# Unread full-height products on TensorE at the start of the two plain attentions of a two-layer kernel

## The chip, the cores and the metric

The kernel runs on one core of a Trainium2 chip. The metric is the device time of one execution, in microseconds (us). Five engines work side by side, each with an instruction list of its own: TensorE (PE: matrix products, with its weight loads shown as PEld), VectorE (DVE), ScalarE (ACT), GpSimd (POOL) and SyncE (SP, which here issues the DMAs). They wait for each other by semaphores. Products are written to PSUM, eight banks of 128 partitions x 512 fp32 values. TensorE's clock is granted at one of two levels, and the profile gives it as a share: 1.00 is 2.4 GHz, 0.50 is 1.2 GHz.

## The reference, cut to what matters

Two pre-norm layers follow each other over 2 x 1024 rows of 128 numbers. Each has an attention of 16 heads of 8 numbers and a mixture of experts. There are three attentions: the layer 0 attention (with rotary embedding), the layer 1 attention, and one with relative positions in the last block. The first two are the plain ones:

```python
scores = jnp.einsum('bqhd,bkhd->bhqk', q, k) * scale
attn = jax.nn.softmax(scores, axis=-1)
out = jnp.einsum('bhqk,bkhd->bqhd', attn, v)
```

With 2 sequences and 16 heads, a plain attention has 32 heads of 1024 x 1024 scores each, and the softmax subtracts each row's maximum.

## The kernel before

The program is one list of stages, the same on all engines: `front(0)` (norm and projections of layer 0), `attention(0)`, `front(1)`, the first experts, `front(2)`, `attention(1)`, `front(3)`, the relative attention, `front(4)`, the second experts. No scheduler moves anything: every engine runs its instructions in the order in which the code writes them, and a wait holds up all that stands behind it on its engine. Between `front(0)` and `attention(0)`, and between `front(2)` and `attention(1)`, there is no meeting of the engines, so each goes on as soon as its own list lets it.

Queries and keys are split into a high and a low part and stacked to 24 rows, stored to DRAM, and loaded head by head by SyncE (`load_qk`) into four slots, four times over in partition blocks of 32. A product of these stacks thus uses 24 or 25 of the 128 rows of the array (thin, below), and products in different blocks of 32 rows run side by side. A product that uses all 128 rows is called full-height.

On TensorE, `attention(a)` first waits for all projections to be read (`products_read`) and for the first head's stacks (`qk_in`). It then computes the scores of heads 0 and 1 ahead of everything else: `scores` (L671) is a pair of thin products of 512 columns each into two banks, for 128 queries against 1024 keys; eight such pairs make a head, 16 the two heads. VectorE takes the maximum of each row over the two banks (`row_max`, L1246) into `M`. The pairs alternate between banks 2, 3 and banks 4, 5, and each waits (`max_done`) until the maximum of the pair before the last is taken. Within head 1's pairs stands `max_row` (L678): a full-height product that turns head 0's maxima into a row. ScalarE copies the row (`MT`), SyncE sends it by DMA into row 24 of the queries' stack, and the head loop's first wait (`m_in`) is for this DMA.

The head loop then calls `position` (L700) for each head. It has eight tiles `kt`. In a tile TensorE computes a score pair of the head after the next (L671), the turned scores of this head with the maximum subtracted by row 24 (`turned`, L686, thin, two products into the ring of banks 0, 1 and 7), and, three tiles behind, the products with the values (`values`, L696: full-height, 256 columns of fp32, four groups of 32 output rows side by side, into columns 0 to 255 of bank 6). ScalarE takes the exponentials of the turned scores (L1529, two per tile). In tile 1 `max_row` turns the next head's maxima. In the first head (`first`) there are no values' products in tiles 0 to 2.

An fp32 product is run as two matmul instructions of two passes each, one of the stacks (whose type is fp32r) as one, so the views count two for a `max_row` and eight for a `values`.

Of the kernel before, what the change touches and what calls it, by code (L numbers as in the profile page):

```python
# [24 lines left out]
P = 128  # L25
# [62 lines left out]
def two_layers(nc, A, out):  # L88
    with ExitStack() as ctx:
        def sb(name, shape, dt=F32):  # L90
            return ctx.enter_context(nc.sbuf_tensor(name, shape, dt))
# [12 lines left out]
        PS = ctx.enter_context(nc.psum_tensor("PS", [P, 8, GW], F32))  # L104

        def bank(b, dt=F32):
            return PS[:, b, :] if dt == F32 else PS[:, b, :].bitcast(dt)
# [12 lines left out]
        ident = sb("ident", [P, P])  # L120
        w_qkv = sb("w_qkv", [P, 3, 5 * P])
# [435 lines left out]
        def _(e):  # L557
# [3 lines left out]
            def products_read(n):  # L561

                e.wait_ge(qin_ok, n)
                e.wait_ge(kin_ok, n)
                e.wait_ge(v_ok, n)
# [4 lines left out]
            def gates(g, bk):  # L570

                for t in range(GT):
                    m = transpose(PS[0:NE1, bk, t * P:(t + 1) * P], gate[:, GT * g + t, :])
                m.then_inc(gtp_ok, 1)

            def front(f):
# [79 lines left out]
                if f == 4:  # L656
                    e.wait_ge(gate_ok, 2)
                    for g in range(NG):
                        if g == NG - 1:
                            e.wait_ge(gate_ok, 3)  # L660
                        gates(g, GATE_BANK[g])

            def attention(a):
                HB = NH * a

                def scores(n, s, qt):

                    e.wait_ge(max_done, 8 * (HB + n) + qt + 1)
                    for kh in range(2):
                        rows_ = slice((2 + kh) * KR, (2 + kh) * KR + MROW)  # L670
                        m = e.matmul(bank(2 + 2 * (qt % 2) + kh), Qs_r[rows_, s, qt * P:(qt + 1) * P],  # L671
                                     Ks_r[rows_, s, kh * GW:(kh + 1) * GW], start=True, stop=True)
                    m.then_inc(s_done, 1)

                def max_row(n, s, alone=False):

                    e.wait_ge(max_done, 2 + 8 * (HB + n) + 8)
                    e.matmul(PS[0:QT, 6, 256:256 + P], M[:, s, :], ident[:], start=alone, stop=True,  # L678
                             skip_group_check=True).then_inc(mt_done, 1)

                def turned(n, s, x, turn):

                    e.wait_ge(exp_done, 16 * (HB + n) + x)
                    rows_ = slice(x % 2 * KR, x % 2 * KR + MROW + 1)
                    kt, qh = x // 2, x % 2
                    e.matmul(bank(RING[(x + turn) % 3]), Ks_r[rows_, s, kt * P:(kt + 1) * P],  # L686
                             Qs_r[rows_, s, qh * GW:(qh + 1) * GW], start=True, stop=True).then_inc(st_done, 1)

                def values(n, s, kt):
                    e.wait_ge(exp_done, 2 + 16 * (HB + n) + 2 * kt + 2)  # L690
                    if kt == 0:
                        e.wait_ge(v_ready, HB + n + 1)
                        if not (isinstance(n, int) and HB + n == 0):
                            e.wait_ge(o_copied, HB + n)
                    for g in range(4):
                        m = e.matmul(PS[32 * g:32 * g + VC, 6, 0:256], Va[:, s, kt, :],  # L696
                                     PR[:, kt % 4, g * 256:(g + 1) * 256], start=(kt == 0), stop=(kt == QT - 1))
                    m.then_inc(pv_done, 1)

                def position(n, block, s, turn, first=False, ahead=True, rows_next=True):  # L700

                    s2 = (s + 2) % SLOTS
                    e.wait_ge(m_in[s], 32 * (NH // SLOTS * a + block + 1))
                    for kt in range(QT):
                        if ahead:
                            if kt == 0:
                                e.wait_ge(qk_in[s2], 128 * (NH // SLOTS * a + block + (s >= 2) + 1))
                            scores(n + 2, s2, kt)
                        turned(n, s, 2 * kt, turn)
                        turned(n, s, 2 * kt + 1, turn)  # L710
                        if kt == 2 and rows_next:
                            e.wait_ge(mt_copied, HB + n + 2)
                        if kt >= 3:
                            values(n, s, kt - 3)
                        elif not first:
                            values(n - 1, (s - 1) % SLOTS, QT - 3 + kt)
                        if kt == 1 and rows_next:
                            max_row(n + 1, (s + 1) % SLOTS, alone=first)

                if a == 0:  # L720
                    e.sem_inc(exp_done, 2)
                    e.sem_inc(pv_done, 4)
                products_read(4 * (a + 1))
                for n in range(2):
                    e.wait_ge(qk_in[n], 128 * (NH // SLOTS * a + 1))
                    for qt in range(QT):
                        scores(n, n, qt)
                        if n == 1 and qt == 1:
                            max_row(0, 0, alone=True)
                e.wait_ge(mt_copied, HB + 1)  # L730
                position(0, 0, 0, 0, first=True)
                for n in range(1, NH):
                    position(n, n // SLOTS, n % SLOTS, n % 3, ahead=n < NH - 2, rows_next=n < NH - 1)
                for kt in range(QT - 3, QT):
                    values(NH - 1, SLOTS - 1, kt)
# [269 lines left out]
            def front2():  # L1005
                back(0)
                front(2)

            plan = [lambda: front(0), lambda: attention(0), lambda: front(1), experts0, front2,
                    lambda: attention(1), lambda: front(3), relative_attention, lambda: front(4), experts1]  # L1010
            for k, run in enumerate(plan):
                run()
# [943 lines left out]
```

## Time and profile before

| | |
|---|---|
| median of 3 runs | 2077.16 us (2076.91 to 2084.83) |
| the profiled execution | 2072.94 us |
| its span, first to last instruction | 2071.1 us |
| TensorE (PE) busy | 1926.4 us, 93% |
| VectorE (DVE) busy | 1376.6 us, 66% |
| ScalarE (ACT) busy | 1206.2 us, 58% |
| mean granted clock of TensorE | 0.952 |

How to read it: the shares of busy time are means over stages with different limits, and a matmul counts as busy while it waits inside the array, so they say little of one stage. What a change in one stage is worth is read from the stretch of the trace in which it lies: which engine is busy there without a break, and who waits for whom. A window of the trace gives for each engine its busy time and its number of instructions in that stretch, and then the mean granted clock. A line of the timeline gives the start, the time from the first start to the last end of a few like instructions in a row, the engine, the line of the code, and what is written from what; in brackets stands the idle time of the engine ahead of it and what ended that.

### The profile page before, as it was taken

Reading aid. Unit: us, or ns where it says so; the run is one execution under the profiler, and the core shown is the slowest. Engines: PE = TensorE matmul, PEld = TensorE weight load, DVE = VectorE, ACT = ScalarE, POOL = GpSimd, SP = SyncE. Lnnn points to the kernel's source line nnn. Section 1 sums busy time; section 2 is a strip of 40 time slices with the busy share of each in tenths; the row PEclk is TensorE's granted clock in tenths of the full one; section 3 lists DMA queues with packets and bytes.
Section 4 is the critical chain, followed back from the end, with each engine's and each line's share of the span. In section 5 each row is a group of like instructions: output and inputs, shape, how many; then the busy total and the mean of one; then the engine's idle time right before and its main releaser. Section 6 shows DMA issues by size and latency. Waiting matters only on the chain.

```text
span 2071.1 us, 40381 instructions
## 1 busy us (share of the span) xinstructions
PE 1926.4 (93%) x13792; PEld 1163.5 (56%) x13792; DVE 1376.6 (66%) x1770; ACT 1206.2 (58%) x2289; POOL 517.3 (25%) x501
## 2 busy tenths in 40 slices
PE   5999999799995999999679999999999999987998
PEld 3333333577772333333456666666666666665887
DVE  5999998456657799997565454545455555336776
ACT  2699999466652699999324444444444444433554
POOL 4000000078872100000122222222222222103654
PEclk8799999799997699999899999999999999988999
DMA  5333333131105233332521122111111211014664
GB/s 168 118 98 107 97 107 106 60 133 64 51 0 172 81 102 101 102 101 78 156 78 48 48 61 54 50 47 47 47 47 52 63 48 50 8 33 172 218 215 145
DMA packets 82558, 182.97 MB, mean 88 GB/s; under 512 B 16048, under 2 KB 45488, under 8 KB 77136
## 3 DMA queue, kind: packets, MB, share of 16 engines
q1 hardware_dynamic: 82448, 181.49, 27.9%
q8 instruction: 71, 1.16, 0.2%
q14 instruction: 39, 0.32, 0.1%
HBM read 146.83 MB, written 36.31 MB: 88 GB/s over the span
## 4 chain that ended last, share of the span: by engine, by line
PE 46%; DVE 2%; SPq 1%; DMA 1%; issue 0%; ACT 0%; DVEq 0%
PE PS L788 17%; PE PS L872 8%; PE PS L800 6%; PE PS L774 6%; PE PS L783 4%; PE PS L763 4%; DVE M L1267 1%; SPq L384 1%; DMA Ks<-in_kv 0%; DMA Ws_r<-w_stack 0%; PE PS L807 0%; PE PS L598 0%; PE PS L746 0%; PE PS L589 0%; PE PS L568 0%
## 5 line engine op out<-in xcount | busy, mean ns | idle before, releaser
L1246 DVE TENSOR_REDUCE M<-PS 128x1 f32<-128x1024 f32 x512 | 595.6, 1219 | 34.1 <-PE PS L671 28.7
L1529 ACT ACTIVATE PR<-PS 128x512 f32<-128x512 f32 x1024 | 539.3, 602 | 52.3 <-PE PS L686 32.3
L1566 ACT ACTIVATE PR<-PS 128x512 f32<-128x512 f32 x512 | 305.8, 598 | 378.5 <-PE PS L788 374.6
L1267 DVE TENSOR_REDUCE M<-PS 128x1 f32<-128x1024 f32 x256 | 312.0, 1222 | 219.4 <-PE PS L774 212.3
L696 PE MATMUL PS<-PR,Va 128*32 128x256 f32 x4096 | 335.7, 401 | 15.8 <-POOL Va L1713 3.6
L686 PE MATMUL PS<-Qs_r,Ks_r 25*128 25x512 f32 x1024 | 311.4, 511 | 0.5 <-ACT PR L1529 0.4
L671 PE MATMUL PS<-Ks_r,Qs_r 24*128 24x512 f32 x1024 | 272.2, 529 | 27.2 <-DMA Ks_r<-k_stack 14.3
L671 PEld LDWEIGHTS PS<-Ks_r,Qs_r 24*128 24x128 f32 x1024 | 100.5, 193 | 236.2 <-issue 162.8
L1262 DVE TENSOR_TENSOR rt<-PS,rel 128x512 f32<-128x512 f32 x128 | 88.5, 691 | 161.0 <-PE PS L746 159.5
L696 PEld LDWEIGHTS PS<-PR,Va 128*32 128x32 f32 x4096 | 83.8, 109 | 151.0 <-issue 63.3
L1713 POOL TENSOR_TENSOR Va<-Vt,nil 128x64 f32<-128x64 f32 x96 | 27.7, 292 | 545.4 <-PE PS L696 542.0
L788 PE MATMUL PS<-BIG_r,Eh 128*128 128x512 f32 x512 | 159.5, 393 | 0.0
L1804 POOL TENSOR_TENSOR qk<-rt 128x512 f32<-128x512 f32 x64 | 82.5, 1288 | 277.4 <-DVE rt L1262 277.4
L686 PEld LDWEIGHTS PS<-Qs_r,Ks_r 25*128 25x128 f32 x1024 | 132.8, 187 | 26.7 <-ACT PR L1529 11.1
L1830 POOL TENSOR_TENSOR BIG_r<-BIG,BIG_r 128x512 fp32r<-128x512 f32 (+1 forms) x96 | 128.5, 1345 | 49.3 <-ACT BIG_r L1598 49.1
L800 PE MATMUL PS<-PR,Va 128*32 128x256 f32 x2048 | 136.8, 385 | 0.0
L1323 DVE TENSOR_TENSOR BIG<-PS,SRC 128x512 f32<-128x512 f32 (+1 forms) x96 | 65.9, 688 | 86.3 <-PE PS L872 86.0
L872 PE MATMUL PS<-Ah,PR_r 128*128 128x512 f32 x376 | 116.4, 391 | 0.0
L872 PE MATMUL PS<-BIG_r,PR_r 128*128 128x512 f32 x384 | 107.9, 390 | 4.1 <-POOL BIG_r L1868 2.9
L788 PEld LDWEIGHTS PS<-BIG_r,Eh 128*128 128x128 f32 x512 | 96.1, 188 | 21.3
L788 PE MATMUL PS<-BIG_r,El 128*128 128x512 f32 x256 | 101.2, 395 | 0.0
L1868 POOL TENSOR_TENSOR BIG_r<-BIG,BIG_r 128x512 fp32r<-128x512 f32 x64 | 82.5, 1291 | 73.4 <-ACT BIG_r L1663 71.4
(202 smaller groups left out, 3065.2 us busy)
## 6 DMA issues: line engine op xcount, KB each, us to landing
Qs<-g_dram SPq DMA_DIRECT2D x29, 1024.0 KB, 4.7
Ks_r<-k_stack SPq DMA_DIRECT2D x256, 100.0 KB
Qs_r<-q_stack SPq DMA_DIRECT2D x256, 96.0 KB
Qs_r<-q_stack SPq DMA_DIRECT2D x128, 128.0 KB
Ks_r<-k_stack SPq DMA_DIRECT2D x128, 128.0 KB
o_dram<-Ob SPq DMA_DIRECT2D x96, 128.0 KB, 2.7
Ks<-g_dram SPq DMA_DIRECT2D x10, 1024.0 KB, 4.9
q_stack<-BIG_r SPq DMA_DIRECT2D x18, 256.0 KB, 3.3
```

The costliest lines, as they stand in the source:

```text
L671: m = e.matmul(bank(2 + 2 * (qt % 2) + kh), Qs_r[rows_, s, qt * P:(qt + 1) * P], Ks_r[rows_, s, kh * GW:(kh + 1) * GW], start=True, stop=True)
L686: e.matmul(bank(RING[(x + turn) % 3]), Ks_r[rows_, s, kt * P:(kt + 1) * P], Qs_r[rows_, s, qh * GW:(qh + 1) * GW], start=True, stop=True). ...
L696: m = e.matmul(PS[32 * g:32 * g + VC, 6, 0:256], Va[:, s, kt, :], PR[:, kt % 4, g * 256:(g + 1) * 256], start=(kt == 0), stop=(kt == QT - 1))
L774: m = e.matmul(bank(bk + kh), q[:, qt * P:(qt + 1) * P], k[:, kh * GW:(kh + 1) * GW], start=first, stop=not first)
L788: m = e.matmul(bank(TURN[kt % 2][qh]), e_part[:, kt * P:(kt + 1) * P], a_part[s][:, qh * GW:(qh + 1) * GW], start=False, stop=(k == 2))
L800: m = e.matmul(PS[32 * g:32 * g + VC, 6, 0:256], Va[:, s, kt, :], PR[:, kt % 4, g * 256:(g + 1) * 256], start=(kt == 0), stop=(kt == QT - 1))
L872: m = e.matmul(out, w[a], h[b], start=start and n == 0, stop=n == 2 or not start, skip_group_check=not start)
L1246: e.tensor_reduce(M[:, s, qt:qt + 1], PS[:, 2 + 2 * (qt % 2):4 + 2 * (qt % 2), :] .rearrange("p a b -> p (a b)"), AX.X, ALU.max, negate=Tr ...
L1267: e.tensor_reduce(M[:, s, qt:qt + 1], PS[:, bk:bk + 2, :].rearrange("p a b -> p (a b)"), AX.X, ALU.max, negate=True).then_inc(max_done, 1)
L1529: e.activation(PR[:, kt % 4, qh * GW:(qh + 1) * GW], bank(RING[(x + turn) % 3]), ACT.Exp, scale=SCALE).then_inc(exp_done, 1)
L1566: e.activation(PR[:, kt % 4, qh * GW:(qh + 1) * GW], bank(TURN[kt % 2][qh]), ACT.Exp)\
L1830: e.tensor_tensor(h0p[0:w, 1, tg % 2, c, :], h0[0:w, c, :], h0p[0:w, 0, tg % 2, c, :].bitcast(F32), ALU.subtract).then_inc(lo_ok, 1)
```

## The change

A helper `keep_warm` is added on TensorE. It multiplies the first columns of the projection weights by the identity matrix, in fp32, with all 128 rows and all 128 output rows, and writes the result to a PSUM bank where nobody reads it. Nothing waits for it and it waits for nothing. It is called in four places of `attention(a)`, in both plain attentions: eight products (attention 0) or twelve (attention 1) of 128 columns ahead of the wait for the projections; one of 256 columns behind each of the 16 score pairs ahead of the head loop, into bank 7; and, in the first head alone, one of 256 columns in tile 0 and one in tile 2, into the columns of bank 6 which the values' products overwrite from tile 3 on. The other engines' code is as it was.

```diff
+            def keep_warm(n, bk=7, cols_=256):
+
+                for _ in range(n):
+                    e.matmul(PS[:, bk, 0:cols_], ident[:], w_qkv[:, 0, 0:cols_], start=True, stop=True)
+
             def attention(a):
                 HB = NH * a
...
                         turned(n, s, 2 * kt, turn)
                         turned(n, s, 2 * kt + 1, turn)
+                        if first and kt == 0:
+                            keep_warm(1, 6)
                         if kt == 2 and rows_next:
                             e.wait_ge(mt_copied, HB + n + 2)
+                            if first:
+                                keep_warm(1, 6)
                         if kt >= 3:
                             values(n, s, kt - 3)
...
                 if a == 0:
                     e.sem_inc(exp_done, 2)
                     e.sem_inc(pv_done, 4)
+                keep_warm([8, 12][a], cols_=P)
                 products_read(4 * (a + 1))
                 for n in range(2):
                     e.wait_ge(qk_in[n], 128 * (NH // SLOTS * a + 1))
                     for qt in range(QT):
                         scores(n, n, qt)
+                        keep_warm(1)
                         if n == 1 and qt == 1:
                             max_row(0, 0, alone=True)
```

## Rows read from the trace of the kernel before

**Rows 1.** The page's costliest groups: busy, mean ns of one, idle before.
```profile
L1246 DVE TENSOR_REDUCE M<-PS 128x1 f32<-128x1024 f32 x512 | 595.6, 1219 | 34.1 <-PE PS L671 28.7
```
**Rows 2.** Windows: busy of PE, PEld, DVE, ACT, POOL (instructions); granted clock.
```profile
39.52:44.42 4.90, 0.00 (x1) 0.00 (x0) 0.44 (x1) 1.74 (x3) 4.90 (x5) 1.00 0.56 176
44.43:47.07 2.64, 0.00 (x0) 0.03 (x1) 0.00 (x0) 0.00 (x0) 2.64 (x9) 0.50 0.84 216
47.07:65.11 18.04, 12.77 (x34) 4.65 (x35) 17.21 (x16) 1.55 (x2) 1.16 (x4) 0.50 0.65 229
...
71.12:81.40 10.28, 10.28 (x76) 3.09 (x73) 6.86 (x6) 6.13 (x12) 0.00 (x0) 0.50 0.16 43
81.97:100.55 18.58, 18.31 (x199) 7.26 (x198) 17.87 (x16) 17.30 (x36) 0.58 (x2) 1.00 0.29 93
...
658.58:678.82 20.24, 12.77 (x35) 4.66 (x35) 18.19 (x16) 1.55 (x2) 1.92 (x3) 0.50 0.74 247
...
684.83:709.44 24.61, 24.61 (x174) 7.30 (x171) 16.66 (x14) 15.36 (x30) 1.97 (x2) 0.50 0.18 57
```
**Rows 3.** Timeline of PE in `front(0)`: start, length, instruction.
```profile
34.14 1.05 PE L647 MATMUL PS<-w_qkv,XT 128*128 128x128 f32 x8
35.03 3.60 PE L642 MATMUL PS<-XT,w_qkv 128*128 128x512 f32 x8
```
**Rows 4.** Windows over three idle stretches of PE elsewhere; granted clock third from last.
```profile
375.55:379.98 4.43, 0.01 (x2) 0.01 (x1) 2.64 (x15) 1.49 (x2) 0.00 (x0) 0.88 0.62 181
...
621.46:626.05 4.59, 0.00 (x1) 0.00 (x0) 2.78 (x16) 1.49 (x2) 0.00 (x0) 0.85 0.00 0
...
1885.88:1888.77 2.89, 0.00 (x1) 0.01 (x1) 2.49 (x4) 1.23 (x2) 1.33 (x2) 1.00 1.02 431
```
**Rows 5.** Timeline, attention 0: the first score pairs; a later one and `max_row`.
```profile
47.07 1.22 PE L671 MATMUL PS<-Ks_r,Qs_r 24*128 24x512 f32 x4 [7.55 <-DMA Ks_r<-k_stack]
...
57.10 0.79 PE L671 MATMUL PS<-Ks_r,Qs_r 24*128 24x512 f32 x2 [0.25 <-DVE M L1246]
57.82 0.60 PE L678 MATMUL PS<-ident,M 128*8 128x128 f32 x2
```
**Rows 6.** Timeline of PE in attention 0's head loop, before and after 81.97.
```profile
71.12 0.79 PE L671 MATMUL PS<-Ks_r,Qs_r 24*128 24x512 f32 x2
...
71.85 1.08 PE L696 MATMUL PS<-PR,Va 128*32 128x256 f32 x8
72.86 0.79 PE L671 MATMUL PS<-Ks_r,Qs_r 24*128 24x512 f32 x2
...
81.40 0.64 PE L678 MATMUL PS<-ident,M 128*8 128x128 f32 x2
81.97 0.50 PE L671 MATMUL PS<-Ks_r,Qs_r 24*128 24x512 f32 x2
...
85.52 0.50 PE L671 MATMUL PS<-Ks_r,Qs_r 24*128 24x512 f32 x2
...
86.52 0.50 PE L671 MATMUL PS<-Ks_r,Qs_r 24*128 24x512 f32 x2
```
**Rows 7.** Timeline of PE in attention 1: first pair, head loop's first, later pairs.
```profile
658.58 1.22 PE L671 MATMUL PS<-Ks_r,Qs_r 24*128 24x512 f32 x4 [6.71 <-DMA Ks_r<-k_stack]
...
678.82 0.79 PE L671 MATMUL PS<-Ks_r,Qs_r 24*128 24x512 f32 x2 [2.63 <-DMA Qs_r<-MT]
...
691.79 0.79 PE L671 MATMUL PS<-Ks_r,Qs_r 24*128 24x512 f32 x2
...
706.12 0.79 PE L671 MATMUL PS<-Ks_r,Qs_r 24*128 24x512 f32 x2
...
710.01 0.50 PE L671 MATMUL PS<-Ks_r,Qs_r 24*128 24x512 f32 x2
```
**Rows 8.** Timeline of PE in the relative attention, at 0.50, behind a thin product.
```profile
1040.73 1.22 PE L774 MATMUL PS<-Ks_r,Qs_r 128*128 128x512 f32 x2
1041.76 1.05 PE L774 MATMUL PS<-XT_r,Ah 128*128 128x512 f32 x2
```

## The prediction

> **What bounds the kernel now.** I read the stretches at the start of the two plain attentions first, then the single instructions in them, and then other places that show the same operations. In a plain attention VectorE's row maximum is the bound: 512 of them at 1219 ns make 595.6 us, with 34.1 us of idle ahead of them [rows 1]. The start is different. In attention 0 TensorE (PE) idles 7.55 us before the first score pair [rows 5]; its granted clock is 1.00 (2.4 GHz) in the first 4.90 us of that and 0.50 (1.2 GHz) in the last 2.64 us [rows 2]. From 47.07 to 65.11 the 16 score pairs of heads 0 and 1 run, at 0.50 all through. PE is busy 12.77 of 18.04 us, VectorE 17.21: each maximum is 18.04 / 16 = 1.13 us after the one before, so VectorE sets this stretch and the half clock costs nothing in it. From 65.11 the head loop runs, and there the half clock does cost: PE is busy 10.28 of 10.28 us from 71.12 to 81.40, VectorE 6.86. A tile (scores and turned scores together, then the values' products) takes 72.86 - 71.12 = 1.74 us [rows 6]; once the clock is back at 81.97 it is 18.58 / 16 = 1.16 us, VectorE's pace again [rows 2]. Attention 1 does the same for longer: idle 6.71 us, first score pair 658.58, head loop 678.82, clock back only at 710.01 [rows 2, 7].
>
> So what can be won is the slow part of the head loops. Attention 0: the first head's tiles start at 65.11, the clock is back at the eleventh; ten tiles in 81.97 - 65.11 = 16.86 us instead of 10 x 1.16 = 11.6, so 5.3 us. Attention 1: 18 tiles in 710.01 - 678.82 = 31.19 us instead of 20.9, so 10.3 us. Together **15.6 us** is the most that a clock held high can give.
>
> **The change, part by part.** It removes nothing and adds only PE instructions; no other engine's list changes. All of it stands or falls with whether the clock is high when the first score pair starts, so that comes first.
>
> *The products in the wait (8 and 12 of 128 columns).* They are not behind the wait but ahead of it, so PE runs them as soon as it has ended its projections. Four such products (128x128 weights, 128 columns, fp32) take 35.03 - 34.14 = 0.89 us at 2.4 GHz [rows 3]; eight take 1.8 us, twelve 2.7. They cost nothing, since the first pair of either attention waits for a DMA [rows 5, 7] that these products do not hold up. They shorten the idle to 7.55 - 1.8 = 5.8 us and 6.71 - 2.7 = 4.0 us. Idle of 4.43 and of 4.59 us elsewhere took the clock down before it ended (the mean over them is 0.88 and 0.85), one of 2.89 us did not (1.00) [rows 4]. The first wait lies beyond the lengths that took it down; the second, 4.0, between the two, nearer the lower row that did. I take it that the clock falls in both.
>
> *The 16 products behind the score pairs, at 1.2 GHz.* One is 256 columns of fp32 against 128x128 weights. From a thin score pair to a full-height product PE needs 57.82 - 57.10 = 0.72 us [rows 5], the same as to the values' product (71.85 - 71.12 = 0.73 [rows 6]). The product itself is bounded by two rows. The values' products, of the same 256 columns but with narrow weights, take 72.86 - 71.85 = 1.01 us until the next score pair starts. Two products with 128x128 weights, behind a thin one as here, take 1041.76 - 1040.73 = 1.03 us until the next full-height one starts [rows 8]; they stream about as long as the added one, which is estimated at 0.90 (half of the 0.90 us of a 512-column product at full clock, 3.60 / 4 [rows 3], doubled for the half clock), and the switch back to thin products adds 0.1 (1.01 - 0.90), so 1.14. The block is then 1.73 to **1.87 us**; I take 1.87, since those weights are of the same size. That is above VectorE's 1.13, so PE becomes the bound of the stretch: 16 x 1.87, and 0.4 for the row of maxima (0.57 from 81.40 to 81.97 [rows 6], less a switch), make 30.3 us. Against 18.04 that is +12.3 us in attention 0 (+10.0 with 1.73). In attention 1 the stretch was 20.24 us [rows 2], since 2.63 us at its end went into waiting for the first head's row of maxima [rows 7]; the longer stretch hides that wait, so +10.1 (+7.8). VectorE can't catch up later, as it is the bound of what follows.
>
> The Trainium skill, in "TensorE: Matmul & The Clock Gate", section "Step-by-step: what each phase is for", says that PE can pull a weight load ahead of running matmuls. By this rule a block would come near its streaming time; the 0.72 us rows, which hold a thin pair and the load behind it, do not agree. It is the last rival.
>
> *The two products in the first head's tiles.* At 1.2 GHz each takes about 0.9 to 1.2 us of PE. The first tiles also wait for ScalarE's exponentials, so part is hidden: 0 to 2.4 us per attention, I take 0.7.
>
> *Does the clock come back sooner?* Then the cost ends early. A block at 1.2 GHz is a thin pair and then a full-height product of 256 columns, with a switch each way: the same sequence as a tile of the head loop, in which four thin products run side by side instead of two. Such tiles left the clock at 0.50 for 10.28 us in attention 0 and 24.61 in attention 1 with PE never idle [rows 2]. It rose right behind a row of maxima that had followed the values' products (81.40, then 0.50 us pairs from 81.97 [rows 6]). Blocks of 1.87 us hold a smaller share of streaming than tiles of 1.74. I take it that they don't raise it, and that it rises in the second or third head as before.
>
> The Trainium skill, in the same page's section "Part 1: The HAM clock gate", says that sustained activity releases the throttle. By this rule blocks that keep PE busy would bring 2.4 GHz back within a few; the trace does not bear that out for this mix of products. It is the second rival.
>
> **Sum.** 12.3 + 10.1 + 2 x 0.7 = 23.8, less 0.7 for a clock that falls only behind the first block in attention 1: **+23 us**. The low ends give 10.0 + 7.8 = 17.8, the high ends 12.3 + 10.1 + 4.8 = 27.2. The profiled execution (2072.94 us, span 2071.1) becomes 2096. The median of the runs shown is 4.2 us above it, and I put the forecast on that: 2077.16 + 23 = **2100**. A head at 1.2 GHz takes 706.12 - 691.79 = 14.33 us [rows 7] against 9.3, so one slow head more or less is 5 us, which is about the spread of the runs (2076.91 to 2084.83). Own range: 2090 (17.8, one head less) to 2114 (27.2, and two heads more).
>
> **Rivals.**
> *Held.* The products are enough and the clock is at 2.4 GHz at the first pair of both attentions. A pair and a full product at that clock take 86.52 - 85.52 = 1.00 us as in the head loop [rows 6], some 0.1 more with wide weights, under VectorE's 1.13: the blocks cost nothing and hold the clock, as the tiles of the loop do. 2077.2 - 15.6 = 2062. For it: only PE's idle lowers the clock in the trace. Against: 5.8 us is longer than any idle that kept it [rows 4]. It decides if 5.8 us of idle leave the clock up. 0.11.
> *Raised by the blocks.* The clock falls but comes back within four blocks: 2 x 4 x 0.74 = 5.9 us lost, 15.6 won, 2067. Against it the tiles at 0.50 above. 0.10, half of it beyond the bound below.
> *Half held.* Only the second wait, of 4.0 us, keeps the clock: 12.3 + 0.7 - 10.3 = +2.7, 2080. 0.06.
> *Raised in the middle.* The row of maxima of head 0, behind the tenth block, raises it, as one does in the head loop: about ten slow blocks in each attention, 2 x 10 x 0.74 = 14.8 lost, 15.6 won, 2076. The row stands behind a full-height product as it does there, but the blocks around it stream less. 0.04. That the products do nothing at all would give about the same time.
> *Loads hidden.* The added product's weights load under the thin pair. Two pairs took 1.22 us against 0.79 for one [rows 5], so a pair streams 0.43; with 0.90 the block is 1.33 us, 32 x 0.2 = 6.4 us lost, less 2.6 for the hidden wait, and 1.4 for the two products: +5, 2082. 0.03.
>
> **How the numbers follow.** The forecast has 0.66. A measurement of this kernel tells some 0.5% (10 us) from no change. Faster by more: 0.11 + 0.05 = 0.16. Within: 0.05 + 0.06 + 0.04 + 0.03 = 0.18. Slower: 0.66. The forecast's own range leaves some 0.05 out; with the cases in the middle and the upper edge of the fast ones, 2064 to 2114 holds 8 in 10.
>
> **What would show it.** Right: in both attentions the granted clock is 0.50 in the stretch between first score pair and head loop, that stretch lasts 28 to 31 us, VectorE is busy in about 60% of it, score pairs start 1.7 to 1.9 us apart. The wait for the first row of maxima in attention 1 is gone. Wrong: the clock at 1.00 at the first pairs (held), or rising behind two to four blocks, or the first pair starting later than 47.1 and 658.6 us. Pairs 1.3 us apart at 0.50 would mean that weights load under thin products.

## The result and the profile after

The changed kernel takes 2107.16 us, the median of 4 runs (2102.84 to 2117.53), against 2079.95 us for the kernel before in its 4 runs (2076.91 to 2084.83). The ratio is 1.0136, 95% interval 1.0091 to 1.0181: **slower by 27 us**. The forecast was 2100, within 2064 to 2114. The profiled execution of after has a span of 2103.2 us (2105.0 us in all) and a mean granted clock of 0.943; that of before had 2071.1 us and 0.952.

All line numbers of TensorE's helpers are five higher than before: L676 is a score pair, L683 `max_row`, L691 the turned scores, L701 the values' products; L666 is `keep_warm`. The maximum of a row is now L1257. Its group on the page of after answers to [rows 1]: busy time, mean of one, idle time ahead.

```profile
L1257 DVE TENSOR_REDUCE M<-PS 128x1 f32<-128x1024 f32 x512 | 600.0, 1220 | 57.7 <-PE PS L676 52.5
```

The 512 maxima take as long as before, but VectorE waits 57.7 us ahead of them instead of 34.1, and 52.5 of that is for score pairs. TensorE holds it up by some 24 us more. Where, the windows of after show (they answer to [rows 2]: busy time and instructions of PE, PEld, DVE, ACT, POOL; then the granted clock, the DMA share and GB/s):

```profile
40.62:46.64 6.02, 1.95 (x18) 1.79 (x17) 0.60 (x2) 1.75 (x3) 6.02 (x10) 0.88 0.67 184
46.64:77.14 30.50, 30.50 (x66) 12.66 (x66) 19.41 (x16) 1.55 (x2) 2.84 (x8) 0.50 0.46 160
77.14:82.42 5.28, 5.28 (x20) 2.24 (x20) 3.87 (x4) 3.39 (x7) 0.00 (x0) 0.50 0.00 0
82.42:123.09 40.67, 40.67 (x281) 12.00 (x281) 27.69 (x23) 25.69 (x50) 0.59 (x2) 0.50 0.19 60
...
673.12:679.82 6.70, 2.85 (x26) 2.68 (x25) 2.20 (x6) 0.00 (x0) 1.04 (x4) 1.00 0.68 186
679.82:710.17 30.35, 30.35 (x67) 12.57 (x67) 19.41 (x16) 1.55 (x2) 9.32 (x6) 0.50 0.54 182
710.17:727.96 17.79, 17.79 (x107) 5.95 (x106) 12.44 (x11) 11.00 (x21) 0.00 (x0) 0.50 0.09 25
```

The second and the sixth line are the score pairs ahead of the two head loops. They took 18.04 and 20.24 us before [rows 2], with VectorE busy in 17.21 and 18.19 us. They take 30.50 and 30.35 us now. VectorE is busy in 19.41 of these, and PE in every one: the bound of the stretch has changed engines. PE is at 0.50 (1.2 GHz) all the while, and also in the line behind, until 123.09 and 727.96.

The timeline of PE in after shows one block after the other, and the ends of the slow time (start, length, instruction; in brackets the idle time ahead):

```profile
40.62 1.95 PE L666 MATMUL PS<-w_qkv,ident 128*128 128x128 f32 x16
46.64 0.79 PE L676 MATMUL PS<-Ks_r,Qs_r 24*128 24x512 f32 x2 [4.07 <-DMA Ks_r<-k_stack]
47.37 1.22 PE L666 MATMUL PS<-w_qkv,ident 128*128 128x256 f32 x2
48.52 0.79 PE L676 MATMUL PS<-Ks_r,Qs_r 24*128 24x512 f32 x2
...
84.16 0.79 PE L676 MATMUL PS<-Ks_r,Qs_r 24*128 24x512 f32 x2
...
123.09 0.64 PE L683 MATMUL PS<-ident,M 128*8 128x128 f32 x2
123.66 0.50 PE L676 MATMUL PS<-Ks_r,Qs_r 24*128 24x512 f32 x2
...
673.12 2.84 PE L666 MATMUL PS<-w_qkv,ident 128*128 128x128 f32 x24
679.82 0.64 PE L676 MATMUL PS<-Ks_r,Qs_r 24*128 24x512 f32 x2 [3.86 <-DMA Ks_r<-k_stack]
680.39 1.22 PE L666 MATMUL PS<-w_qkv,ident 128*128 128x256 f32 x2
681.54 0.79 PE L676 MATMUL PS<-Ks_r,Qs_r 24*128 24x512 f32 x2
...
710.17 0.79 PE L676 MATMUL PS<-Ks_r,Qs_r 24*128 24x512 f32 x2
...
717.18 0.79 PE L676 MATMUL PS<-Ks_r,Qs_r 24*128 24x512 f32 x2
...
727.96 0.50 PE L676 MATMUL PS<-Ks_r,Qs_r 24*128 24x512 f32 x2
...
737.15 0.50 PE L676 MATMUL PS<-Ks_r,Qs_r 24*128 24x512 f32 x2
```

The products in the wait leave 4.07 and 3.86 us of idle. In attention 0 the clock falls in that idle (0.88 is the mean over it and the products), in attention 1 it is 1.00 over the whole wait and falls in the first pair, which takes 0.64 us, between the 0.50 of a pair at 2.4 GHz and the 0.79 of one at 1.2. From then on a block (a thin pair and the full-height product behind it) is 48.52 - 46.64 = 1.88 us: 0.73 from the pair to the full-height product, 1.15 back.

**Where the 32.1 us between the two spans went.** The traces can be laid beside each other at the same tile of the program. Attention 0: the first pair starts 0.43 earlier (46.64 against 47.07), the stretch is 12.46 longer, and the head loop's first 26 tiles take 123.66 - 77.14 = 46.52 us against 100.55 - 65.11 = 35.44 [rows 2], +11.08. Up to that tile: +23.1. From there to attention 1's first pair 1.9 us are won back (679.82 against 658.58 is +21.2). Attention 1: stretch +10.11, the first 18 tiles 737.15 - 710.17 = 26.98 us against 31.19 [rows 7], -4.2. Together +27.1. The other 5.0 us lie behind that tile, 4.6 of them from `front(3)` on (its first product starts at 1024.90 against 997.38), in stages where no instruction differs; in the 75.2 us from the first product of `front(3)` the mean granted clock is 0.73 in after and 0.82 in before. I did not follow these up; they are of this pair of executions, and the medians differ by 27.2.

### The profile page after: what moved, and what is told of

Read it like the earlier page. It is cut to its first block, busy times and chain, and to the rows that moved or that the text cites. A ratio compares the mean times of both kernels' runs of the same rounds, so it can differ in the third digit from the quotient of the medians.

```text
span 2103.2 us, 40603 instructions
## 1 busy us (share of the span) xinstructions
PE 1977.5 (94%) x13904; PEld 1187.1 (56%) x13904; DVE 1380.7 (66%) x1770; ACT 1207.0 (57%) x2289; POOL 517.8 (25%) x501
## 4 chain that ended last, share of the span: by engine, by line
PE 46%; DVE 2%; DMA 1%; SPq 1%; issue 0%; ACT 0%; DVEq 0%
PE PS L799 17%; PE PS L883 8%; PE PS L785 6%; PE PS L811 6%; PE PS L794 4%; PE PS L774 4%; SPq L384 1%; DVE M L1278 0%; DMA Ks<-in_kv 0%; DMA Ws_r<-w_stack 0%; PE PS L818 0%; PE PS L598 0%; PE PS L757 0%; PE PS L589 0%; DMA k_stack<-PR_r 0%
## 5 line engine op out<-in xcount | busy, mean ns | idle before, releaser
L1257 DVE TENSOR_REDUCE M<-PS 128x1 f32<-128x1024 f32 x512 | 600.0, 1220 | 57.7 <-PE PS L676 52.5
L701 PE MATMUL PS<-PR,Va 128*32 128x256 f32 x4096 | 339.2, 405 | 16.2 <-POOL Va L1724 8.2
L691 PE MATMUL PS<-Qs_r,Ks_r 25*128 25x512 f32 x1024 | 311.1, 516 | 0.0
L676 PE MATMUL PS<-Ks_r,Qs_r 24*128 24x512 f32 x1024 | 275.8, 534 | 7.9 <-DMA Ks_r<-k_stack 7.9
L676 PEld LDWEIGHTS PS<-Ks_r,Qs_r 24*128 24x128 f32 x1024 | 101.1, 194 | 226.4 <-issue 176.1
L701 PEld LDWEIGHTS PS<-PR,Va 128*32 128x32 f32 x4096 | 84.1, 109 | 152.7 <-issue 79.8
L691 PEld LDWEIGHTS PS<-Qs_r,Ks_r 25*128 25x128 f32 x1024 | 132.2, 188 | 24.2 <-ACT PR L1540 8.7
L799 PE MATMUL PS<-Ah,Eh 128*128 128x512 f32 x256 | 100.8, 394 | 0.0
```

The costliest lines, as they stand in the source:

```text
L799: m = e.matmul(bank(TURN[kt % 2][qh]), e_part[:, kt * P:(kt + 1) * P], a_part[s][:, qh * GW:(qh + 1) * GW], start=False, stop=(k == 2))
L1257: e.tensor_reduce(M[:, s, qt:qt + 1], PS[:, 2 + 2 * (qt % 2):4 + 2 * (qt % 2), :] .rearrange("p a b -> p (a b)"), AX.X, ALU.max, negate=Tr ...
```

## The experiments

Each kernel is the changed one with the edit shown; all compute the whole result, since the added products are read by nobody. The theory: the blocks at 1.2 GHz are the loss, and they are at 1.2 GHz because the products ahead don't cover the wait. The rivals: the products in the wait or in the tiles cost the time; the blocks cost it at any clock, by the array or by PSUM; the clock can't be held here by any such products.

### The three parts alone

Only the products in the wait (no blocks, no tile products):

```diff
-                        if first and kt == 0:
-                            keep_warm(1, 6)
...
-                            if first:
-                                keep_warm(1, 6)
...
                         scores(n, n, qt)
-                        keep_warm(1)
```

> Of the change only the 8 and 12 products ahead of the wait are left. If the loss comes from the blocks at 1.2 GHz, the clock still falls in both waits (4.1 and 3.9 us of idle are left, as in the changed kernel), the 16 score pairs go at VectorE's 1.13 us again, and the time is that of before within 0.3% or so, save a head more or less at the low clock (5 us). If the products in the wait themselves delay something, the time lies above before by up to 20 us. If they held the clock, the first pairs would run at 1.00.

Measured: 2079.66 us against 2080.12, ratio 0.9997 (0.9968 to 1.0026). The idle left is 4.12 us, and the stretch is what it was in [rows 2], at 0.50:

```profile
44.41:62.40 17.99, 12.77 (x34) 4.62 (x34) 17.16 (x16) 1.55 (x2) 2.82 (x8) 0.50 0.65 229
```

Only the blocks:

```diff
-                keep_warm([8, 12][a], cols_=P)
...
-                        if first and kt == 0:
-                            keep_warm(1, 6)
...
-                            if first:
-                                keep_warm(1, 6)
```

> Only the 16 products behind the score pairs. If these carry the loss, the stretch from first pair to head loop takes 30.4 us in both attentions against 18.0 and 20.2, pairs start 1.87 us apart, and the kernel is slower than before by 20 to 30 us, as the whole change is. If the two products in the first head's tiles carry it, the time is near that of before.

Measured: 2107.87 us, ratio 1.0144 (1.0076 to 1.0212), some 30 us. A window over 29.61 us of the stretch in attention 0, PE busy in all of it, at 0.50 (the head loop's first pair starts at 77.89, 30.50 us behind the first pair, and in attention 1 it is 30.50 us too):

```profile
47.39:77.00 29.61, 29.61 (x65) 12.42 (x66) 18.52 (x16) 1.55 (x2) 0.74 (x3) 0.50 0.47 163
```

Only the tile products:

```diff
-                keep_warm([8, 12][a], cols_=P)
...
                         scores(n, n, qt)
-                        keep_warm(1)
```

> Only the two products in the first head's tiles 0 and 2. If ScalarE's exponentials set the pace of these tiles, the two cost nothing to 1.5 us per attention and the time is that of before within 5 us either way. The rival: they change how long the clock stays low behind them, seen as the rise at another head than before (5 us for each head).

Measured: 2082.54 us, ratio 0.9995 (0.996 to 1.0029). Tile 0 and tile 4 of the first head in attention 0:

```profile
62.61 0.79 PE L676 MATMUL PS<-Ks_r,Qs_r 24*128 24x512 f32 x2 [0.43 <-DVE M L1255]
...
69.62 0.79 PE L676 MATMUL PS<-Ks_r,Qs_r 24*128 24x512 f32 x2
```

The four tiles take 7.01 us, 1.0 more than the 6.01 from 65.11 to 71.12 before [rows 2, 6], which is too little for the times to show. So the blocks alone are the loss that the times show; the other two parts, alone, change them by nothing that can be measured.

### A wait that is filled

More products in the wait, all else as in after:

```diff
-                keep_warm([8, 12][a], cols_=P)
+                keep_warm([26, 28][a], cols_=P)
```

> The whole change, but with 26 and 28 products in the wait instead of 8 and 12: 26 x 0.22 = 5.8 us and 28 x 0.22 = 6.2 us, so that nearly all of the wait (6.0 to 7.6 and 6.7 us) is filled and less than 2 us of idle are left. If the low clock is the only thing wrong with the blocks, the clock is 1.00 from the first pair on, pairs start 1.13 us apart, the head loop begins some 18 us behind the first pair and runs at 1.16 us a tile at once: 15 us faster than before, about 2065. If the blocks cost TensorE time at any clock, or the high clock does not last through the score pairs, the kernel is as slow as the changed one.

Measured: 2076.58 us, ratio 0.998 (0.9942 to 1.0019), runs from 2063.26 to 2093.53: by time, undecided. The profile shows why; it is a window and the timeline of PE:

```profile
46.62:64.38 17.76, 17.57 (x68) 7.87 (x68) 17.21 (x16) 1.55 (x2) 2.68 (x8) 1.00 0.70 240
```

```profile
46.62 0.50 PE L676 MATMUL PS<-Ks_r,Qs_r 24*128 24x512 f32 x2 [0.23 <-DMA Ks_r<-k_stack]
47.06 0.70 PE L666 MATMUL PS<-w_qkv,ident 128*128 128x256 f32 x2
47.69 0.50 PE L676 MATMUL PS<-Ks_r,Qs_r 24*128 24x512 f32 x2
...
653.36 0.50 PE L676 MATMUL PS<-Ks_r,Qs_r 24*128 24x512 f32 x2 [1.52 <-DMA Ks_r<-k_stack]
...
655.90 1.22 PE L666 MATMUL PS<-w_qkv,ident 128*128 128x256 f32 x2
657.05 0.79 PE L676 MATMUL PS<-Ks_r,Qs_r 24*128 24x512 f32 x2
```

In attention 0 only 0.23 us of idle is left. PE is at 1.00 (2.4 GHz) through the stretch; a block takes 1.07 us, VectorE is busy in 17.21 of 17.76 us, and the stretch is as short as before the change. This is the same change at the other clock: the blocks cost nothing there. In attention 1, 1.52 us of idle was left; the clock was still high in the first two blocks and fell in the third.

Still more products:

```diff
-                keep_warm([8, 12][a], cols_=P)
+                keep_warm([32, 36][a], cols_=P)
```

> As e4_hold, with 32 and 36 products in the wait: 7.1 and 8.0 us, so that no idle is left ahead of the first pair in either attention (in e4_hold 1.52 us of idle ahead of attention 1 were followed by the fall of the clock behind the third pair). If idle ahead of the pairs is what takes the clock down, it is 1.00 through both stretches, both take 17.8 us, and the time is 15 us or more under that of before (2060 to 2066), a first pair up to 1 us later set against it. If the pairs with their products can't keep the clock up by themselves, it falls somewhere in the stretch in one attention or both, and the time stays at 2070 to 2085.

Measured: **2057.44 us against 2074.06, ratio 0.9898 (0.9836 to 0.996)**, faster. Two windows, the stretches ahead of both head loops, and PE's timeline at the head loop of attention 1:

```profile
45.18:62.90 17.72, 17.55 (x67) 7.85 (x67) 17.19 (x16) 1.55 (x2) 1.62 (x5) 1.00 0.68 231
...
651.32:669.30 17.98, 17.55 (x67) 7.84 (x66) 17.45 (x16) 1.55 (x2) 1.40 (x3) 1.00 0.75 259
```

```profile
669.82 0.50 PE L676 MATMUL PS<-Ks_r,Qs_r 24*128 24x512 f32 x2 [0.85 <-DMA Qs_r<-MT]
...
670.26 0.94 PE L666 MATMUL PS<-w_qkv,ident 128*128 128x256 f32 x2
671.13 0.79 PE L676 MATMUL PS<-Ks_r,Qs_r 24*128 24x512 f32 x2
```

Both stretches are held, at VectorE's pace. Nothing but the number of products differs from after, which is slower by some 49 us (0.9898 against 1.0136); so the rival by which the blocks cost their time whatever the clock is out, and the clock can be held. One fall is left, in the product that starts at 670.26, behind 0.85 us of idle in which the head loop waits for the first head's row of maxima.

The filled wait without blocks and tile products, run once, tells whether they do anything for it:

```diff
-                keep_warm([8, 12][a], cols_=P)
+                keep_warm([32, 36][a], cols_=P)
...
-                        if first and kt == 0:
-                            keep_warm(1, 6)
...
-                            if first:
-                                keep_warm(1, 6)
...
                         scores(n, n, qt)
-                        keep_warm(1)
```

> The same full wait, but without the products behind the pairs and in the tiles. If these are needed to keep the clock up, it falls within a few pairs of the first, the pairs go at VectorE's 1.13 us all the same, and the time is that of before (2070 to 2090). If the wait is all that matters, the clock stays at 1.00 and the time is 2062.

Measured: 2075.53 us, one run, which by time lies within those of before. In its profile the clock is high at the first pair and falls behind the fifth (the first line here counts two pairs), in attention 1 behind the sixth:

```profile
45.51 0.74 PE L676 MATMUL PS<-Ks_r,Qs_r 24*128 24x512 f32 x4
...
49.59 0.52 PE L676 MATMUL PS<-Ks_r,Qs_r 24*128 24x512 f32 x2 [0.63 <-DVE M L1252]
50.73 0.79 PE L676 MATMUL PS<-Ks_r,Qs_r 24*128 24x512 f32 x2 [0.62 <-DVE M L1252]
```

A wait that is filled is not enough: in both attentions the clock fell among thin pairs with 0.6 us of idle between them. With the blocks it stayed through both stretches.

### The size of a block

Blocks of half the columns, all else as in after:

```diff
                         scores(n, n, qt)
-                        keep_warm(1)
+                        keep_warm(1, cols_=P)
```

> The whole change with 128 columns instead of 256 behind each pair. At 1.2 GHz the product streams 0.43 us less, so pairs should start 1.87 - 0.43 = 1.44 us apart: the stretch takes 23.5 us instead of 30.4, which is 5.4 us over before in attention 0 and 1 to 3 us in attention 1 (where the wait for the row of maxima hides a part), some 8 us in all, against 22 of the whole change. If the loss came with the number of products and not with their length, it would stay near 20 us.

Measured: 2087.85 us, ratio 1.0038 (0.9994 to 1.0081), some +8 us with an interval that just reaches no change. Window and timeline:

```profile
46.55:70.23 23.68, 23.68 (x66) 12.68 (x66) 18.98 (x16) 1.55 (x2) 2.95 (x9) 0.50 0.60 209
```

```profile
46.55 0.80 PE L676 MATMUL PS<-Ks_r,Qs_r 24*128 24x512 f32 x2 [3.95 <-DMA Ks_r<-k_stack]
47.28 0.80 PE L666 MATMUL PS<-w_qkv,ident 128*128 128x128 f32 x2
48.01 0.79 PE L676 MATMUL PS<-Ks_r,Qs_r 24*128 24x512 f32 x2
```

A block is 1.46 us, still above VectorE's 1.13, and the stretch 23.68. So 128 columns of fp32 less take 1.88 - 1.46 = 0.42 us off the block at 1.2 GHz, and 1.46 - 1.13 = 0.33 us a pair is still lost. The loss goes with the size of the block, as it must if the block bounds the stretch.

### A burst in place of all that

No products in the wait and no blocks. Eight of 256 columns in a row between the last score pair and the head loop, while PE runs at 1.2 GHz; the tile products stay:

```diff
-                keep_warm([8, 12][a], cols_=P)
...
                         scores(n, n, qt)
-                        keep_warm(1)
                         if n == 1 and qt == 1:
                             max_row(0, 0, alone=True)
+                keep_warm(8)
                 e.wait_ge(mt_copied, HB + 1)
```

> No products in the wait and behind the pairs; instead eight of 256 columns one behind the other (6.8 us at 1.2 GHz) between the last pair and the head loop, and the two in the first tiles. If full-height products without a thin one between them raise the clock, it is 1.00 behind them in both attentions: they cost 6 us in attention 0 and 4 in attention 1 (which waits 2 us there anyway) and save 15.6, so 5 us or more faster than before. If the clock stays at 0.50 behind them, the kernel is 10 us slower than before.

Measured: **2065.42 us against 2074.06, ratio 0.995 (0.9922 to 0.9978)**, faster, and its 10 runs lie between 2060.92 and 2068.77, where those of before lie between 2064.91 and 2094.25. The last pair in attention 0, and windows over the burst and the start of the head loop behind it, in attention 0 and in attention 1:

```profile
63.43 0.79 PE L676 MATMUL PS<-Ks_r,Qs_r 24*128 24x512 f32 x2 [0.34 <-DVE M L1256]
```

```profile
64.15:69.38 5.23, 5.23 (x19) 4.09 (x17) 1.48 (x2) 0.00 (x0) 0.00 (x0) 0.69 0.39 122
69.38:87.00 17.62, 17.22 (x169) 7.11 (x168) 16.92 (x15) 16.06 (x33) 0.29 (x1) 1.00 0.19 65
675.92:682.44 6.52, 6.52 (x18) 5.00 (x16) 1.48 (x2) 0.00 (x0) 5.68 (x5) 0.55 0.41 131
682.44:700.00 17.56, 17.16 (x169) 7.09 (x168) 16.85 (x15) 15.99 (x33) 3.98 (x3) 1.00 0.19 58
```

Full-height products alone raise the clock within the burst, in both attentions: means of 0.69 and 0.55 over a burst that begins at 0.50 and ends at 1.00 put the rise at 67.4 and 681.8. Both head loops start at 2.4 GHz. It isn't free: VectorE is busy in 1.48 of the 5.23 us in attention 0, and the loop starts 69.38 - 63.43 = 5.95 us after the last pair, where before it was one pair's 1.13 or so. What it buys is worth more, since from there on the clock is 1.00 to the end of both attentions.

### The last fall, and the tile products

The filled wait, and in attention 1 four products ahead of the head loop's wait, to cover the 0.85 us:

```diff
-                keep_warm([8, 12][a], cols_=P)
+                keep_warm([32, 36][a], cols_=P)
...
                             max_row(0, 0, alone=True)
+                keep_warm([0, 4][a])
                 e.wait_ge(mt_copied, HB + 1)
```

> As e5_fill, with four more products of 256 columns (1.7 us at 2.4 GHz) in attention 1 behind the last pair, where in e5_fill PE idled 0.85 us for the row of maxima and the clock then fell at the start of the head loop. If it was this idle on top of the light blocks that let the clock fall there, it now stays at 1.00 through attention 1 too, and two to three heads are 5 us shorter each: 10 us or so under e5_fill, less 0.9 for the longer wait, near 2050. If the first tiles themselves are too light to keep the clock, it falls there as before and the time stays at 2057.

Measured: 2059.32 us against 2078.15, ratio 0.9927 (0.989 to 0.9964). In the profiled execution (2053.59 us) the clock never falls in either attention; VectorE's idle ahead of the maxima is down to 19.9 us. A page group and two windows:

```profile
L1258 DVE TENSOR_REDUCE M<-PS 128x1 f32<-128x1024 f32 x512 | 594.4, 1218 | 19.9 <-PE PS L676 14.6
```

```profile
32.30:370.00 337.70, 327.36 (x3294) 136.81 (x3292) 305.33 (x275) 286.57 (x582) 20.73 (x47) 1.00 0.35 111
636.50:981.00 344.50, 329.55 (x3314) 139.30 (x3312) 311.01 (x301) 288.90 (x585) 21.31 (x41) 1.00 0.34 109
```

Two of its 10 runs are near 2077, with a mean granted clock of 0.961 where the other eight have 0.967 to 0.977, so the hold isn't certain. The four added products can't be told from none by the times: the intervals of this kernel and the one with the filled wait alone overlap, and the 10 us that were expected between them do not show in the times.

The same without the tile products (the edit is against the kernel above):

```diff
-                        if first and kt == 0:
-                            keep_warm(1, 6)
...
-                            if first:
-                                keep_warm(1, 6)
```

> e9_fill_wait without the two products in the first head's tiles. These tiles have no products with the values until tile 3. If the two are needed to bridge them at 2.4 GHz, the clock falls within the first head in one attention or both and the time is some 5 to 20 us above e9_fill_wait; if they are not, the times are the same.

Measured: 2079.41 us, ratio 0.9991 (0.9948 to 1.0034): the gain is gone. PE's timeline in the first head of attention 0, and a window behind:

```profile
63.94 0.49 PE L676 MATMUL PS<-Ks_r,Qs_r 24*128 24x512 f32 x2 [0.53 <-DVE M L1254]
...
66.29 0.67 PE L676 MATMUL PS<-Ks_r,Qs_r 24*128 24x512 f32 x2 [0.65 <-DVE M L1254]
...
67.91 0.79 PE L676 MATMUL PS<-Ks_r,Qs_r 24*128 24x512 f32 x2
```

```profile
66.90:100.00 33.10, 33.10 (x232) 9.60 (x228) 23.18 (x20) 21.45 (x42) 0.59 (x2) 0.50 0.19 61
```

The first head's tiles 0 to 2 hold no values' products. Without the two added ones the clock was high through the stretch and fell there, at tile 3, in attention 1 too (in the values' products at 688.23). The two cost 1.0 us an attention at 1.2 GHz (the third experiment); with the wait filled, the whole gain hangs on them.

## Why the prediction was right

**The clock falls in both waits.** Right in attention 0; in attention 1 it falls just behind the wait, in the first pair. The idle left in attention 0 was 4.07 us, not 5.8: the eight products took 1.95 us as worked out (1.8), but in this execution the wait itself was shorter (40.62 to 46.64, 6.0 us, where before had 7.55 [rows 5]). The DMA that ends it varies, with first pairs at 44.41 to 47.39 us in the traces of the first two experiments. The outcome was right, but its reason, the length of the idle, was weaker than it looked. 4.07 and 3.86 us both lie beyond the 2.89 us that kept the clock [rows 4], yet the trace of before also has an idle of 2.53 us, in `front(2)`, which lost it; the prediction left it out:

```profile
639.47:642.00 2.53, 0.00 (x1) 0.03 (x1) 2.53 (x9) 0.78 (x1) 2.06 (x2) 0.95 0.77 240
```

From 642.20 to 645.00 the clock is 0.50 there. With the falls behind 1.52 and 0.85 us in the experiments, this step came out in part by luck.

**The block bounds the stretch.** Right, and to the size: 1.87 us forecast at the wide weights' end, 1.88 measured; +12.3 and +10.1 us forecast, +12.46 and +10.11 measured. That attention 1 loses less because the wait for the row of maxima is hidden shows in the line at 710.17, which has no idle in brackets, where before had 2.63 us [rows 7]. It was undone by taking the blocks out (0.9997) and by raising the clock (0.9898).

**The late fall in attention 1.** It happened, in the first pair, and the first block took 681.54 - 679.82 = 1.72 us: 0.15 won, not 0.7.

**The two tile products.** Right in sign and near in size: 0.7 us an attention was taken of 0 to 2.4, and 1.0 was measured. The first four tiles took 84.16 - 77.14 = 7.02 us in attention 0 and 717.18 - 710.17 = 7.01 in attention 1, where before had 6.01 both times (65.11 to 71.12 and 678.82 to 684.83 [rows 2, 6, 7]). The third experiment shows the same 1.0 without the longer stretch.

**Where the clock comes back.** This term was mis-sized. "The second or third head as before" was the fourth in attention 0 (behind the `max_row` at 123.09, 26 tiles instead of 10) and the second in attention 1 (10 instead of 18). Without the tile products that is 11.08 - 1.01 = +10.1 and -4.2 - 1.0 = -5.2 us in this execution: two slow heads more and one less, at the 5 us a head of the prediction. The sum of its other parts, 12.46 + 10.11 + 1.01 + 1.00, is 24.6, against the 23 forecast. The medians differ by 27.2. That this is so near the forecast is luck in so far as it also holds the place of the return, and what I did not follow up behind attention 1. Of the 18 rises seen inside the head loops of these traces, 13 stood right behind a `max_row` that followed values' products, as the prediction read from [rows 6], and the other 5 came within the tile behind one; but rows at 94.44 and 108.77 us passed without one. What decides which of them raises the clock is open.

**The rivals.** *Held* was the right mechanism with too few products: 2062 was forecast for it, and the filled wait gives 2057.44, 16.6 us under the median of before beside it (the most was put at 15.6). Its point of decision, "if 5.8 us of idle leave the clock up", was rightly doubted. *Raised by the blocks* and *Raised in the middle* fall with the 30.50 us at 0.50 in which PE never idles. There the Trainium skill, in "TensorE: Matmul & The Clock Gate", section "Part 1: The HAM clock gate", says that sustained activity releases the throttle; the trace of after does not agree for blocks of thin and full-height products, and the burst, of full-height products alone, agrees. *Half held* fell with the clock at 0.50 from 680.4 on. *Loads hidden* would have given blocks of 1.33 us. The same page's section "Step-by-step: what each phase is for" lets a weight load run ahead beside matmuls where the row groups don't conflict or the load goes to the background weight buffer. The 0.73 us from thin pair to full product is what it was before, so no run here shows it behind a thin pair; among the full-height products in the wait it is seen, with 1.79 us of loads (PEld) and 1.95 of products in a window of 6.02 us of which PE idles 4.07.

## What to carry to other kernels

A product that only keeps TensorE busy was free here at 2.4 GHz and dear at 1.2: find the clock at the place where it would run before you add it. If the clock falls ahead of it, fill the wait that lets it fall, to the end, and price the same products at both levels (1.07 and 1.88 us here, beside a neighbour that needs 1.13). Where a wait's length varies from run to run, a row of full-height products just ahead of the work that needs the clock costs some us of its own (5.95 in attention 0 here where 1.13 stood) but raised it in both places of the one execution that was traced.

## What the runs showed of the hardware that was not expected

- An idle stretch needn't be long for the clock to fall behind it: 1.52 us in attention 1 of the kernel with 26 and 28 products, 0.85 us in the one with 32 and 36, and 2.53 us in `front(2)` before, where 2.89 us ahead of other work kept it [rows 4]. The length of the idle stretch alone, by which the prediction argued, doesn't tell. That the idle is the cause in the first two is not shown: with the 0.85 us filled one trace has no fall, but the times don't confirm it.
- The same block of a thin pair and a full-height product held 2.4 GHz through 17.72 us when it found it with no idle ahead, and did not bring it back in 30.50 us when it found 1.2. With 1.52 us of idle ahead it found 2.4 GHz and lost it in the third block. So the level at which it runs depended on what was there before.
- The kernel before spreads over 29 us from run to run (2064.91 to 2094.25). Its mean granted clock goes with the time: 0.955 to 0.958 in the three runs under 2066 us, 0.938 in the two at 2094. The traces of these kernels differ in the head in which the clock comes back, at 14.33 against some 9.3 us a head; with the burst, which fixes that place, the spread is 8 us. That the place of the return makes the spread of before fits this, but only one of its runs was traced.
